# Masked attention on one core: late blocks moved in halves, with the diagonal blocks copied by GpSimd

## The reference, cut to what matters

```python
h = max(layernorm(x), 0)                       # x: 4096 x 256, f32
adj = maximum(adj, eye)                        # 4096 x 4096
q, k, v = h @ Wqs[head], h @ Wks[head], h @ Wvs[head]        # 8 heads of 64
scores = q @ k.T * 64 ** -0.5 + 0.01 * eye - 1e16 * (1 - adj)
att = softmax(scores, axis=-1)
out = x + sum over heads of att @ v @ Wo[head]
```

## Time and profile before

| what | us |
|---|---|
| median of three runs | 2877.41 (2876.8 to 2883.67) |
| the profiled execution | 2880.15 |
| its span, first to last instruction | 2878.4 |
| TensorE matmuls busy | 2703.1 (94%) |
| VectorE busy | 2237.4 (78%) |
| ScalarE busy | 1843.9 (64%) |
| GpSimd busy | 1494.5 (52%), of it 1006.0 the issue of late moves |
| mean granted TensorE clock | 0.979 |

### The profile page before, as it was taken

One profiled execution on the slowest core, in us unless ns is written; L12 is line 12 of the kernel. 1 busy time (PEld: TensorE's weight loads), 2 busy tenths in 40 slices (PEclk: granted clock), 3 DMA queues, 4 the chain that ended last, 5 costly groups with the idle time before them and its releaser, 6 DMA issues. The chain is left out here.

```text
span 2878.4 us, 58579 instructions
## 1 busy us (share of the span) xinstructions
PE 2703.1 (94%) x17344; PEld 1907.5 (66%) x17344; DVE 2237.4 (78%) x3833; ACT 1843.9 (64%) x3041; POOL 1494.5 (52%) x2706
## 2 busy tenths in 40 slices
PE   7999999999999999999898999999999999999997
PEld 5666666666666676666655766666676666667664
DVE  6778787887787788878657877777887787888784
ACT  4566666766666676666545666666666666666664
POOL 2255565546555454656324555655545565554553
PEclk9999999999999999999999999999999999999999
DMA  5256665556566555656435555666556565654653
GB/s 157 75 137 144 135 155 128 130 133 145 138 140 151 131 132 126 150 133 150 127 97 117 122 141 131 151 137 140 137 124 143 128 154 137 139 137 120 145 133 101
DMA packets 258750, 384.95 MB, mean 134 GB/s; under 512 B 98432, under 2 KB 119424, under 8 KB 258688
## 3 DMA queue, kind: packets, MB, share of 16 engines
q0 software_dynamic: 107520, 218.26, 33.7%
q1 hardware_dynamic: 148992, 161.76, 22.3%
q10 hardware_dynamic: 2176, 4.19, 0.4%
HBM read 169.87 MB, written 12.71 MB: 63 GB/s over the span
## 5 line engine op out<-in xcount | busy, mean ns | idle before, releaser
L665 DVE CUSTOM_DVE_ANT_0 S<-psS,B 128x1024 f32<-128x1024 f32 x1024 | 1221.8, 1216 | 475.3 <-PE psS L408 239.0
L266 POOL DMA_DIRECT2D S<-S x2048 | 1006.0, 500 | 1074.5 <-DVE S L686 1031.8
L552 ACT ACTIVATE S<-S,negm 128x1024 f32<-128x1024 f32 (+1 forms) x768 | 1096.8, 1428 | 20.0 <-DVE negm L672 19.9
L559 ACT ACTIVATE PT<-psT 128x512 f32<-128x512 f32 x1024 | 607.0, 593 | 631.6 <-PE psT L421 619.8
L408 PE MATMUL psS<-K,QH 128*128 128x512 f32 x2048 | 737.0, 441 | 58.6 <-DVE mx L665 56.2
L421 PE MATMUL psT<-ident,S 128*128 128x128 f32 x4096 | 644.2, 281 | 7.3 <-ACT S L552 4.9
L408 PE MATMUL psS<-K,QL 128*128 128x512 f32 x2048 | 649.9, 399 | 0.0
L421 PEld LDWEIGHTS psT<-ident,S 128*128 128x128 f32 x4096 | 485.9, 142 | 247.3 <-issue 154.6
L686 DVE STREAM_TRANSPOSE S<-S 128x2048 f32<-128x2048 f32 x256 | 590.4, 2307 | 1.6 <-PE psO L444 0.9
L444 PE MATMUL psO<-S,V 128*64 128x256 f32 x4096 | 512.6, 394 | 74.9 <-DMA S<-S 74.8
L431 PE MATMUL psO<-PT,V 128*64 128x256 f32 x4096 | 521.8, 386 | 0.0
(11 more groups left out here) (51 smaller groups left out, 991.1 us busy)
## 6 DMA issues: line engine op xcount, KB each, us to landing
S<-S SPq DMA_DIRECT2D x2048, 64.0 KB, 2.7
S<-S POOLq DMA_DIRECT2D x2048, 64.0 KB, 2.5
B<-in_adj POOLq DMA_DIRECT2D x256, 256.0 KB, 6.6
hq<-hT_scratch SPq DMA_DIRECT2D x32, 256.0 KB, 3.5
RB<-rden_scratch SPq DMA_DIRECT2D x128, 64.0 KB, 3.3
S<-in_x SPq DMA_DIRECT2D x8, 512.0 KB, 3.6
hT_scratch<-S ACTq DMA_DIRECT2D x8, 512.0 KB, 4.4
acc<-in_x POOLq DMA_DIRECT2D x16, 256.0 KB, 7.5
```

Of the source, the lines that this page charges most:

```text
L266: pool.dma_start(dst, src).then_inc(late_sent[q], 16)
L552: nc.scalar.activation(part, part, ACT.Exp, bias=negm[:, h % 2, q:q + 1], accum_out=sums[:, h % 2, q, e:e + 1]).then_inc(probs_ready, 1)
L559: nc.scalar.activation(PT[:, s % RING, :], psT[s % 2][:, :], ACT.Copy).then_inc(pt_act, 1)
L665: nc.vector.tensor_tensor_reduce(out=part, in0=psS[j % 2][:, :], in1=B[:, q, k * SLOT:(k + 1) * SLOT], scale=SCALE, scalar=LOWEST, op0=ALU ...
```

## The change: what it does

- Moves in halves. Both queues issue the moves of a q sorted by the destination quadrant: first those into quadrants 0 and 1 (half 0), then those into 2 and 3 (half 1); the staging area is ordered by the same quadrant, so a half is one slot of it. Each half has semaphores of its own. The mask of slot 4 waits for half 0 of q = 0, slot 5 for half 1, slots 6 and 7 for the halves of q = 1.
- The four moves of distance 0 (quadrant onto itself) are no DMAs any more. GpSimd copies them with four `tensor_copy` of 32 x 512 f32, after it has issued its four moves of distance 2, and then waits for its own copies.
- VectorE: the late transpose of q = 0 goes ahead of the masks of slots 0 and 1 of the head after next; before it stood between them.
- TensorE: in the last period both transposes come before both slots of scores; all 32 late instructions come after the four periods, ahead of values 4 to 7.

```diff
-SP_MOVES = [(i, (i + d) % QUAD) for d in (1, 3) for i in range(QUAD)]
-POOL_MOVES = [(i, (i + d) % QUAD) for d in (0, 2) for i in range(QUAD)]
+HALVES = 2
+SP_MOVES = [[((j - d) % QUAD, j) for j in range(2 * half, 2 * half + 2) for d in (1, 3)] for half in range(HALVES)]
+POOL_MOVES = [[((j - d) % QUAD, j) for j in range(2 * half, 2 * half + 2) for d in (2,)] for half in range(HALVES)]
+MOVED, SENT = 16 * len(SP_MOVES[0]), 16 * len(POOL_MOVES[0])
+KEPT = QUAD // HALVES
+def staged_in(j):
+    return divmod(j - SPT, HALVES)
...
             for q in range(QT):
                 sp.wait_ge(late_transposed, count(i, h, QT, q + 1))
-                for qi, qj in SP_MOVES:
-                    src, dst = late_blocks(h, q, qi, qj)
-                    sp.dma_start(dst, src).then_inc(late_moved[q], 16)
+                for half in range(HALVES):
+                    for qi, qj in SP_MOVES[half]:
+                        src, dst = late_blocks(h, q, qi, qj)
+                        sp.dma_start(dst, src).then_inc(late_moved[q][half], 16)
...
-        def move_late(i, h, q):
+        def move_late(i, h, q, converted=None):
             wait_apart(pool, late_transposed, count(i, h, QT, q + 1), pool_passed)
-            for qi, qj in POOL_MOVES:
-                src, dst = late_blocks(h, q, qi, qj)
-                pool.dma_start(dst, src).then_inc(late_sent[q], 16)
+            for half in range(HALVES):
+                for qi, qj in POOL_MOVES[half]:
+                    src, dst = late_blocks(h, q, qi, qj)
+                    pool.dma_start(dst, src).then_inc(late_sent[q][half], 16)
+            if converted is not None:
+                wait_apart(pool, bias_ready, converted, pool_passed)
+            for qi in range(QUAD):
+                src, dst = late_blocks(h, q, qi, qi)
+                nc.gpsimd.tensor_copy(dst, src).then_inc(late_kept, 1)
+            wait_apart(pool, late_kept, count(i, h, QT * QUAD, (q + 1) * QUAD), pool_passed)
...
-            move_late(i, h, 0)
+            move_late(i, h, 0, i * SLOTS + SLOTS if h == 0 else i * SLOTS + SLOTS + 6 if adj_rest else None)
...
                 for q in range(QT):
-                    pe.wait_ge(late_moved[q], count(i, h, 16 * len(SP_MOVES), 16 * len(SP_MOVES)))
-                    pe.wait_ge(late_sent[q], count(i, h, 16 * len(POOL_MOVES), 16 * len(POOL_MOVES)))
+                    for half in range(HALVES):
+                        pe.wait_ge(late_moved[q][half], count(i, h, MOVED, MOVED))
+                        pe.wait_ge(late_sent[q][half], count(i, h, SENT, SENT))
+                pe.wait_ge(late_kept, count(i, h, QT * QUAD, QT * QUAD))
...
                     transposes(i, h, 2 * c + e)
-                    pair_scores(i, h, c, nxt, nxt2, e)
+                    if c < PERIODS - 1:
+                        pair_scores(i, h, c, nxt, nxt2, e)
+                if c == PERIODS - 1:
+                    for e in range(2):
+                        pair_scores(i, h, c, nxt, nxt2, e)
...
                     values(i, h, 3)
-                    values_late(i, h, range(LATE_FIRST))
...
-            values_late(i, h, range(LATE_FIRST, LATE))
+            values_late(i, h, range(LATE))
...
-            if not first:
-                for tq in range(QT):
-                    if j == t1_first_slot(tq):
-                        dve.wait_ge(late_moved[tq], count(i, h, 16 * len(SP_MOVES), 0))
-                        dve.wait_ge(late_sent[tq], count(i, h, 16 * len(POOL_MOVES), 0))
+            if not first and j >= SPT:
+                tq, half = staged_in(j)
+                dve.wait_ge(late_moved[tq][half], count(i, h, MOVED, 0))
+                dve.wait_ge(late_sent[tq][half], count(i, h, SENT, 0))
+                dve.wait_ge(late_kept, count(i, h, QT * QUAD, tq * QUAD + (half + 1) * KEPT - QT * QUAD))
...
+            if nxt:
+                transpose_late(i1, h1, 0, True)
             if nxt2:
                 mask(i2, h2, 0)
-            if nxt:
-                transpose_late(i1, h1, 0, True)
-            if nxt2:
                 mask(i2, h2, 1)
             if nxt:
                 transpose_late(i1, h1, 1, True)
```

More of the change, by code:

```diff
@@ L49 @@
 NE = len(PIECES)
-LATE_FIRST = LATE // 2
 START = 1
@@ L62, in count @@
     return i * (GROUP * per) + (h * per + extra)
-def t1_first_slot(q):
-    return SPT + (N - (QT - q) * LATE * P) // SLOT
+def staged_in(j):
+    return divmod(j - SPT, HALVES)
 def ring_used(s):
@@ L109, in group_programs @@
     dve_passed, pool_passed = sem(f"dve_passed{g}"), sem(f"pool_passed{g}")
-    late_moved = [sem(f"late_moved{g}{q}") for q in range(QT)]
-    late_sent = [sem(f"late_sent{g}{q}") for q in range(QT)]
+    late_moved = [[sem(f"late_moved{g}{q}{half}") for half in range(HALVES)] for q in range(QT)]
+    late_sent = [[sem(f"late_sent{g}{q}{half}") for half in range(HALVES)] for q in range(QT)]
     adj_in = [[sem(f"adj_in{g}{q}{k}") for k in range(SPT)] for q in range(QT)]
@@ L114, in group_programs @@
      transposed, pt_act, pt_free, o_ready, projected, summed, den_ready, head_added,
-     late_transposed, late_used, odd_copied, o_summed, rden_stored, rden_in) = (
+     late_transposed, late_kept, late_used, odd_copied, o_summed, rden_stored, rden_in) = (
         sem(f"{s}{g}") for s in (
@@ L118, in group_programs @@
             "probs_ready", "transposed", "pt_act", "pt_free", "o_ready", "projected", "summed", "den_ready",
-            "head_added", "late_transposed", "late_used", "odd_copied", "o_summed",
+            "head_added", "late_transposed", "late_kept", "late_used", "odd_copied", "o_summed",
             "rden_stored", "rden_in"))
@@ L168, in group_programs @@
     if not norm:
-        late_used_before, late_moved_before, late_sent_before, slot_masked_before, projected_before, o_summed_before, head_added_before = before
+        late_used_before, late_moved_before, late_sent_before, late_kept_before, slot_masked_before, projected_before, o_summed_before, head_added_before = before
     def sync_program(sp):
@@ L187, in sync_program @@
             for q in range(QT):
-                sp.wait_ge(late_moved_before[q], 16 * len(SP_MOVES) * STEPS)
-                sp.wait_ge(late_sent_before[q], 16 * len(POOL_MOVES) * STEPS)
+                for half in range(HALVES):
+                    sp.wait_ge(late_moved_before[q][half], MOVED * STEPS)
+                    sp.wait_ge(late_sent_before[q][half], SENT * STEPS)
+            sp.wait_ge(late_kept_before, QT * QUAD * STEPS)
         for w, dst in ((Wk, wk), (Wv, wv)):
@@ L737, in step @@
                 mask(i1, h1, 7)
-            if nxt2:
-                mask(i2, h2, 0)
             if nxt:
@@ L742, in step @@
             if nxt2:
+                mask(i2, h2, 0)
                 mask(i2, h2, 1)
@@ L775, in group_programs @@
     return ((sync_program, gpsimd_program, tensor_program, scalar_program, vector_program),
-            (late_used, late_moved, late_sent, slot_masked, projected, o_summed, head_added))
+            (late_used, late_moved, late_sent, late_kept, slot_masked, projected, o_summed, head_added))
 def build(nc, x, adj, Wk, Wq, Wv, Wo, out):
```

## The result

The changed kernel takes 2889.73 us (median of ten runs) against 2878.35 of the kernel before on the same chip: ratio 1.0036, 95% interval 1.0025 to 1.0047, that is slower by 0.4%. The forecast was 2738, its range 2704 to 2800.

The account below looks back on a forecast made before the run. TensorE's own work bounds most steps; h = 2 wastes 165 us waiting for late moves. From 2880.15: -165, -4, +5, +12, +13, net -139, gives 2741, or 2738 us against the median; range 2704 to 2800.

Parts of the forecast that it names:

- What bounds the kernel: Step h = 2 wastes 5.5 us on average waiting for late moves; 30 such steps, 165 us within reach.
- Part 1: Late transpose ahead of two masks, late values last: moves start 2.6 us earlier in the first half, 1.2 in the second.
- Part 2: Waits for moves by halves: narrowest margin 2.2 us in h = 2; 0.17 us a step taken, 5 us in all.
- neither gains: The added waits, 8 on VectorE and 5 on TensorE a step, were taken at 0 cost.
- Part 3: GpSimd copies for four DMAs a half: 0.57 us a copy, +0.8 us a step on GpSimd, 13 us in all.
- I take 0.45: New stall in h = 3, mask of slot 6 waiting for GpSimd's conversion: 0.45 us, 30 times, 13 us.
- one drain each half of some 0.1: GpSimd's wait for its own copies after each half, put at some 0.1 us.
- My own rule: Sensitivity of GpSimd's chain: each 0.1 us on a copy adds 1.6 us a pair.
- Rivals B and C: Copies cost 0.8 us (2849 us, chance 0.15), or 1.05 us with GpSimd bounding h = 2 and 3 (2969, chance 0.06).
- Rival A: GpSimd's copies overlap or cost under 0.5 us and it keeps ahead: 2708 us, chance 0.13.
- VectorE beside the copies: Diagonal's addition and reciprocal product slowed beside GpSimd's copies: 0.2 us in an even step, 62 times, 12 us.

Follow-up runs that it names:

- x9: The changed kernel with GpSimd's copies cut to one element a partition in h = 2 and h = 3; 2725.03 us, ratio 0.9451.
- x4: The kernel before with the two reorderings of VectorE and TensorE alone, whole waits and diagonal by DMA; 2784.61 us, ratio 0.9651.
- x1: The changed kernel with its diagonal blocks moved by GpSimd DMAs again, halves and reorderings kept; 2756.93 us, ratio 0.9564.
- x2: The changed kernel with the diagonal blocks neither copied nor moved; 2724.24 us, ratio 0.9447.
- x14: The kernel before with each set's moves issued sorted by destination quadrant, same moves and whole waits; 2913.32 us, ratio 1.0106.
- x11: The changed kernel with GpSimd's wait for its own copies only behind the second half; 2831.4 us, ratio 0.9828.
- x10: The changed kernel with GpSimd's copies cut to one element a partition in h = 0 and h = 1; 2875.06 us, ratio 0.9967.

## Why the prediction was wrong, step by step

**What bounds the kernel: right.** h = 2 wasted 5.57 us over h = 0 by the means (26.05 less 20.48), 5.5 forecast, and it could be had: x9 has 20.57 there.

**Part 1, the reordering: right.** In the odd step from 1053.60 the late transposes stand where they were put:

```profile
1065.46 2.30 DVE L703 STREAM_TRANSPOSE S<-S 128x2048 f32<-128x2048 f32 x1
...
1070.80 2.31 DVE L703 STREAM_TRANSPOSE S<-S 128x2048 f32<-128x2048 f32 x1 [0.77 <-PE psO L458]
```

That is +11.9 and +17.2 for 12.6 and 17.3. The late transpose of q = 0 ends at +14.2 (14.9 forecast). The reordering alone gives 3.5% (x4). What Part 1 did not see is that the conversions of h = 3 move up to VectorE's two-operand instructions: 0.7 to 0.9 us of h = 3 in x1, x2 and x4.

**Part 2, the halves: half right.** With the reordering they add: x4 0.9651, x1 0.9564, intervals apart. The issue order that they bring was taken for free ("neither gains"), and costs about 33 us in the kernel before (x14). Its term was missing. (It was measured in the old order only.)

**Part 3, the copies: the step that failed.** The mechanism was written down, the conversions of h = 3 behind GpSimd's longer program, with "I take 0.45" for the stall. It is 5.7 us (24.54 for 18.81), 172 us over 30 pairs where the sum had 13. The copy itself was sized well:

```profile
L277 POOL COPY S<-S x1024: 599/608/892, 102.5 to 2867.6; 32x512 f32<-32x512 f32 x171
```

608 ns at the median, 570 forecast; four in a row take 2.6 to 2.8 us for 2.3. The rest of the half was not: "one drain each half of some 0.1" (0.2 in the sum of the chain) is 0.68 to 0.8 us ahead of the next moves, as a rule, and 0.8 ahead of the loads; only ahead of a conversion is it 0.30. It stands as POOL S L272 <- POOL S L277 in the waits, and such a half costs 5.4 us where I had 4.5. GpSimd enters h = 3 at +2.7 on average (forecast +0.5; the two halves of h = 2 at 0.9 each are 1.8 of these 2.2 us). From its first move there to the first conversion it needs 10.4 us in 25 of 30 pairs (forecast 9.0), 11.1 in one and 12.4 to 12.7 in four, where its timeline has a gap of some 2 us among the moves, listed as issue. So the conversions begin at +13.3, 3.8 us later than forecast (+9.5), and with the 0.45 that is some 4.3 of the 5.7 us. The rest is a term that the forecast put at nothing: TensorE's clock. TensorE waits for 3.7 us of an h = 3, and its busy time rises by 2.1, from 18.8 to 20.9: 0.7 of it in the steps of full clock too, and another 1.7 in the 25 of 30 where the granted clock fell, 1.4 on average. The prediction read this share off the old stall of h = 2 and gave the new stall none. My own rule, each 0.1 us on a copy adds 1.6 us a pair, should have told me that the range could not end at 2800 with a cost that no row showed: the drain had no bounds at all, and by these rows it is over half of the 0.9 us by which a half was dearer than forecast; dropping one wait in two brings back 58 us (x11). Rivals B and C had the right place and an unlikely condition (a dear copy), while a dear wait gave the same.

Rival A is refuted. The four copies lie in four quadrants and take 0.65 us each, one behind the other; the Trainium skill's page "GPSIMD Engine Reference", section 2.1, by which cores that are done go on to the next instruction, gives no overlap that these rows show.

**VectorE beside the copies: right in kind and size.** h = 0 lost 0.42 us (0.2 forecast, in both even steps: 12 us; x10, with tiny copies in h = 0 and 1, is 15 us faster than the change). The diagonal's addition and the product with the reciprocals in the step from 1115.51, beside the copies of 1119.73:

```profile
1120.05 0.43 DVE L688 TENSOR_TENSOR S<-S,diag 128x128 f32 x1 [0.17 <-DVE mx L682]
...
1121.10 0.84 DVE L720 TENSOR_TENSOR O<-Oodd,RB 64x256 f32<-64x256 f32 x1 [0.23 <-DVE Oodd L715]
```

They take 0.29 and 0.42 us undisturbed. The Trainium skill, "GPSIMD Engine Reference", section 8, warns of just this, VectorE instructions with two SBUF inputs; the trace agrees.

## What to carry to other kernels

Work that is taken off a shared resource (here DMAs) and given to a serial engine is priced by that engine's whole program up to the next thing that someone waits for, with every wait of the engine for itself in it; an engine at 56% on average had in h = 2 a chain that ran 2.7 us past the step's end, of work (15.31 of 20.44 us) and of waits for its own copies and for loads. A new stall is to be priced with the clock that it may cost TensorE. A cost that no row shows needs bounds even when it looks like small change, and most of all where it stands four times in the chain. And try the reordering by itself first: it brought 3.5% with no new instruction, the whole change nothing, and without the copies 4.4%.

## What was not expected of the hardware

GpSimd's wait for its own copies costs 0.75 us (median) behind the last one's end where moves follow, longer than a copy (0.61), and 0.30 where a conversion follows. A VectorE addition of 293 ns with two SBUF operands took up to 2423 ns in the changed kernel, 1076 before. The 2423 stand beside two conversions, to whose end it lasted; beside copies alone these instructions took 0.86 us at most there. The order in which 16 moves between partition quadrants are issued is worth 1.1% of the kernel before. Without any diagonal transfer h = 3 still took 19.55 us (x2), and 18.99 with tiny copies in their place (x9): in x9 GpSimd comes to the conversions later and the two instructions lose 0.14 us a step beside them, in x2 0.87.
